# Attention block of a fused tokenizer, attention and expert kernel: softmax denominators as a column beside the values, weighted sums transposed back, divided, and transposed again

## What is computed

```python
qkv = (xn @ w_qkv + b_qkv).reshape(b, t, 3, H, hd)      # b=64, t=82, H=16, hd=16
scores = jnp.einsum('bhqd,bhkd->bhqk', q, k) * scale
attn = jax.nn.softmax(scores + bias, axis=-1)           # bias depends on q-k and the head
out = jnp.einsum('bhqk,bhkd->bhqd', attn, v)
out = jnp.transpose(out, (0, 2, 1, 3)).reshape(b, t, dim)
h = h + out @ w_out + b_out
```

## Time and profile before

| what | value |
|---|---|
| median of runs | 857.1 us |
| profiled execution: time, span | 861.1 us, 859.3 us |
| mean granted clock of TensorE over the span | 0.91 |
| busy: PE, PEld, DVE, ACT, POOL | 690.2, 527.5, 599.7, 349.9, 285.6 us |
| attention passes 0 to 63 | from 241.2 us to 657.0 us of the span |

### The profile page before, as it was taken

The page is one execution under the profiler, slowest core; times in us unless marked ns, Lnnn a source line. Parts: engine busy times, 40 slices in busy tenths (PEclk is TensorE's granted clock), DMA queues, the critical chain, the costliest instruction groups (busy, mean ns, idle before and its releaser), DMA issues. The chain is left out here.

```text
span 859.3 us, 24631 instructions
## 1 busy us (share of the span) xinstructions
PE 690.2 (80%) x10030; PEld 527.5 (61%) x10030; DVE 599.7 (70%) x1199; ACT 349.9 (41%) x793; POOL 285.6 (33%) x361
## 2 busy tenths in 40 slices
PE   1769696461479999999999999999988479999960
PEld 1657543320257777777777777777766368888850
DVE  0627657843459899999899998998885246766525
ACT  1211111000035555555555555555454335555533
POOL 2474200002272333333233333332000455667333
PEclk9879899675779999999999999999998769999995
DMA  8990100005910000000000000000000412222117
GB/s 158 225 311 8 37 1 0 1 12 178 306 23 8 15 16 14 15 16 21 14 9 21 15 15 16 15 15 15 21 14 15 98 56 74 71 81 76 51 65 272
DMA packets 34786, 51.42 MB, mean 60 GB/s; under 512 B 9044, under 2 KB 26292, under 8 KB 34548
## 3 DMA queue, kind: packets, MB, share of 16 engines
q1 hardware_dynamic: 29524, 39.57, 16.2%
q0 software_dynamic: 5152, 10.29, 4.2%
HBM read 36.91 MB, written 18.00 MB: 64 GB/s over the span
## 5 line engine op out<-in xcount | busy, mean ns | idle before, releaser
L934 ACT ACTIVATE probT<-psP 82x328 f32<-82x328 f32 x256 | 112.1, 438 | 161.4 <-PE psP L834 161.4
L993 DVE TENSOR_REDUCE mx<-psS 82x8 f32<-82x656 f32 x128 | 106.5, 832 | 42.4 <-PE psS L825 42.2
L834 PE MATMUL psP<-ident_all,prob 82*82 82x82 f32 x1024 | 117.3, 236 | 22.5 <-ACT probT L934 22.4
L834 PEld LDWEIGHTS psP<-ident_all,prob 82*82 82x82 f32 x1024 | 89.8, 120 | 65.6 <-issue 25.9
L755 POOL TENSOR_TENSOR h_flat<-h_flat,po 128x256 f32<-128x256 f32 x41 | 29.7, 725 | 263.7 <-ACT po L921 263.7
L995 DVE TENSOR_TENSOR prob<-psS,mx 82x656 f32<-82x656 f32 x128 | 107.1, 837 | 4.4
L926 ACT ACTIVATE prob<-prob 82x656 f32<-82x656 f32 x128 | 94.8, 741 | 3.1 <-DVE prob L995 3.1
L802 PE MATMUL psQ<-hT,early 128*128 128x328 f32 x256 | 83.1, 449 | 0.6 <-ACT hT L903 0.5
L1005 DVE RECIPROCAL rden<-psO 128x164 f32<-128x164 f32 x64 | 74.8, 1169 | 4.4 <-PE psO L852 4.4
L812 PE MATMUL psQ<-early,hT 128*82 128x256 f32 x256 | 66.7, 383 | 0.1
L825 PE MATMUL psS<-kT,qT 32*82 32x82 f32 x2048 | 53.6, 242 | 0.0
(11 more groups left out here) (218 smaller groups left out, 1216.5 us busy)
## 6 DMA issues: line engine op xcount, KB each, us to landing
img<-in_x SPq DMA_DIRECT2D x6, 1008.0 KB, 19.5
out<-h_flat SPq DMA_DIRECT2D x41, 128.0 KB, 2.5
fused_rows<-in_txt SPq DMA_DIRECT2D x1, 4928.0 KB, 25.1
h_flat<-entry_rows SPq DMA_DIRECT2D x6, 512.0 KB, 6.5
h_flat<-fused_rows SPq DMA_DIRECT2D x1, 2176.0 KB, 16.2
ex_w2a<-in_ff_w_A SPq DMA_DIRECT2D x1, 2048.0 KB, 11.2
ex_w1b<-in_ff_w_B SPq DMA_DIRECT2D x2, 1024.0 KB, 16.7
out<-h_flat SPq DMA_DIRECT2D x8, 256.0 KB, 4.8
```

Of the source, the lines that this page charges most:

```text
L834: mm = te.transpose(psP[0:T, s * T:s * T + T], prob[:, b % 2, g, s, :], ident_all[0:T, 0:T])
L934: act.activation(probT[:, b % 2, g, :, :].rearrange("p s t -> p (s t)"), psP[0:T, 0:4 * T], ACT.Copy).then_inc(S["probT_ready"], 1)
L993: v.tensor_reduce(mx[:, half, :, :], s4, X, ALU.max).then_inc(S["max_ready"], 1)
```

## The change

The values of a head now have 32 columns on the stationary side: 16 values and 16 ones (the memset of vv writes 1.0 and the copy fills the first 16). One matmul per head gives the sums and the denominator, and `one2` and its 16 matmuls are gone. The result in psO has channels on partitions; ACT copies it to oT, PE transposes it in four pieces of 128 columns back to psO (tokens on partitions), DVE takes the reciprocal of one column per head (82x16) and multiplies (82x256) into att, PE transposes that in two pieces, and ACT copies it to attT, where the projection reads it as before. On DVE normalise now stands ahead of read_qk.

The core of the diff:

```diff
-                te.wait_ge(S["att_ready"], b)
-                for t in range(2):
-                    for a in range(2):
-                        for g in range(HG):
-                            te.matmul(psO[32 * g:32 * g + 32, t * T:t * T + T], vv[:, b % 4, 4 * t + g, a, :],
-                                      probT[:, b % 2, g, 2 * t + a, :], start=(a == 0), stop=(a == 1), tile_position=(0, 32 * g))
-                for t in range(2):
-                    for a in range(2):
-                        for g in range(HG):
-                            mm = te.matmul(psO[32 * g:32 * g + 32, (2 + t) * T:(3 + t) * T], one2[:, a, :],
-                                           probT[:, b % 2, g, 2 * t + a, :], start=(a == 0), stop=(a == 1), tile_position=(0, 32 * g))
+                te.wait_ge(S["attT_ready"], b)
+                for h in range(NH):
+                    k, s = h % 4, h // 4
+                    mm = te.matmul(psO[32 * k:32 * k + 32, s * T:s * T + T], vv[:, b % 4, h, :],
+                                   probT[:, b % 2, h % 8 // 2, 2 * (h // 8) + h % 2, :], start=True, stop=True, tile_position=(0, 32 * k))
                 mm.then_inc(S["weigh_done"], 1)
+            def turn_back(b):
+                te.wait_ge(S["oT_ready"], b + 1)
+                for s in range(4):
+                    mm = te.transpose(psO[0:T, s * 128:s * 128 + 128], oT[:, s, :], ident_all[:])
+                mm.then_inc(S["back_done"], 1)
+            def turn_att(b):
+                te.wait_ge(S["att_ready"], b + 1)
+                for c in range(2):
+                    mm = te.transpose(psO[:, c * T:c * T + T], att[:, 8 * c:8 * c + 8, :].rearrange("p h d -> p (h d)"), ident_all[0:T, 0:T])
+                mm.then_inc(S["attT_ps"], 1)
             def project(n):
-                te.wait_ge(S["att_ready"], last_of[n] + 1)
+                te.wait_ge(S["attT_ready"], last_of[n] + 1)
...
+            def copy_oT(b):
+                act.wait_ge(S["weigh_done"], b + 1)
+                act.activation(oT[:].rearrange("p s t -> p (s t)"), psO[:, 0:4 * T], ACT.Copy).then_inc(S["oT_ready"], 1)
+            def copy_attT(b):
+                act.wait_ge(S["attT_ps"], b + 1)
...
+                    ins = act.activation(attT[:, :, a:a + size], psO[:, 0:2 * T].rearrange("p (c t) -> p c t", c=2)[:, :, lo:lo + size], ACT.Copy)
+                ins.then_inc(S["attT_ready"], 1)
...
             def normalise(b):
-                v.wait_ge(S["weigh_done"], b + 1)
...
-                v.reciprocal(rden[:], o3[:, 1, :, :]).then_inc(S["rden_ready"], 1)
+                v.wait_ge(S["back_done"], b + 1)
+                v.wait_ge(S["attT_ps"], b)
+                o3 = psO[0:T, :].rearrange("p (h e) -> p h e", h=NH)
+                v.reciprocal(rden[:], o3[:, :, HD:HD + 1]).then_inc(S["rden_ready"], 1)
                 v.wait_ge(S["rden_ready"], b + 1)
-                for a, lo, size in pieces(T * b, T, RA):
-                    ins = v.tensor_tensor(attT[:, :, a:a + size], o3[:, 0, :, lo:lo + size], rden[:, :, lo:lo + size], ALU.mult)
-                ins.then_inc(S["att_ready"], 1)
+                v.tensor_tensor(att[:], o3[:, :, 0:HD], rden[:].to_broadcast([T, NH, HD]), ALU.mult).then_inc(S["att_ready"], 1)
```

More of the change, by code:

```diff
@@ L682, in attention_block @@
         wrel = sb("wrel", [128, 2, 2, 2]); own = sb("own", [128, 2]); ownq = sb("ownq", [128, 2])
-        one2 = sb("one2", [T, 2, 32])
         bown = sb("bown", [128, 2, 4])
@@ L690, in attention_block @@
         qT = sb("qT", [128, 2, 2, 2, QT]); kT = sb("kT", [128, 2, 2, 2, QT])
-        vv = sb("vv", [T, 4, 8, 2, 32])
+        vv = sb("vv", [T, 4, NH, 32])
         mx = sb("mx", [T, 2, 2, 4])
         prob = sb("prob", [T, 2, HG, 4, T]); probT = sb("probT", [T, 2, HG, 4, T])
-        attT = sb("attT", [128, 2, RA]); rden = sb("rden", [128, 2, T])
+        oT = sb("oT", [128, 4, T]); att = sb("att", [T, NH, HD])
+        attT = sb("attT", [128, 2, RA]); rden = sb("rden", [T, NH, 1])
         po = sb("po", [128, 2, C])
@@ L710, in _ @@
             sp.dma_start(out_row[:], row(I["at_b_out"], 128)).then_inc(S["a_w_in"], 16)
-            for name, tile in (("qrel", qrel), ("kt0", kt0), ("kt1", kt1), ("wrel", wrel), ("own", own), ("one2", one2)):
+            for name, tile in (("qrel", qrel), ("kt0", kt0), ("kt1", kt1), ("wrel", wrel), ("own", own)):
                 sp.dma_start(tile[:], I[name]).then_inc(S["a_w_in"], 16)
@@ L729, in _ @@
             pool.memset(mhalf[:], -0.5).then_inc(S["mhalf2_set"], 1)
-            pool.memset(vv[:], 0.0).then_inc(S["vv_clear"], 1)
+            pool.memset(vv[:], 1.0).then_inc(S["vv_ones"], 1)
             pool.wait_ge(S["mhalf2_set"], 1)
@@ L772, in _ @@
             te.wait_ge(S["bvb_ready"], 1)
-            te.wait_ge(S["a_w_in"], 16 * 8)
+            te.wait_ge(S["a_w_in"], 16 * 7)
             for c in range(2):
@@ L882, in _ @@
                     qk(b // 4 + 1, b % 4)
+                if 0 <= b - 2 < NB:
+                    turn_back(b - 2)
                 if 0 <= b - 1 < NB:
@@ L886, in _ @@
                     val(b + 1)
+                if 0 <= b - 2 < NB:
+                    turn_att(b - 2)
                 if b < NB:
@@ L911, in copy_val @@
                     act.wait_ge(S["weigh_done"], b - 3)
-                v4 = bank(("val", b))[0:T, 0:C].rearrange("p (s a d) -> p s a d", s=8, a=2)
-                pair = vv[:, b % 4, :, :, :].rearrange("p s a (h d) -> p s (a h) d", h=2)[:, :, 0:4:3, :]
-                act.activation(pair, v4, ACT.Copy).then_inc(S["psQ_act"], 1)
+                act.activation(vv[:, b % 4, :, 0:HD], bank(("val", b))[0:T, 0:C].rearrange("p (h d) -> p h d", h=NH),
+                               ACT.Copy).then_inc(S["psQ_act"], 1)
+            def copy_oT(b):
[3 more added lines that the diff above has]
+                act.wait_ge(S["attT_ps"], b + 1)
+                done = (T * b + T - RA + 127) // 128
+                if done > 0:
+                    act.wait_ge(S["project_done"], done)
+                for a, lo, size in pieces(T * b, T, RA):
+                    ins = act.activation(attT[:, :, a:a + size], psO[:, 0:2 * T].rearrange("p (c t) -> p c t", c=2)[:, :, lo:lo + size], ACT.Copy)
+                ins.then_inc(S["attT_ready"], 1)
             def copy_project(n):
@@ L938, in _ @@
                 copy_xT(n)
-            act.wait_ge(S["vv_clear"], 1)
+            act.wait_ge(S["vv_ones"], 1)
             copy_val(0)
@@ L943, in _ @@
             for b in range(NB + 3):
+                if 0 <= b - 2 < NB:
+                    copy_oT(b - 2)
                 if 0 <= b - 1 < NB:
@@ L955, in _ @@
                     copy_val(b + 1)
+                if 0 <= b - 2 < NB:
+                    copy_attT(b - 2)
                 if b < NB:
@@ L1013, in _ @@
                 normal_stats(n)
-            v.wait_ge(S["a_w_in"], 16 * 8)
+            v.wait_ge(S["a_w_in"], 16 * 7)
             v.tensor_scalar(ownq[:], own[:], float(HD) ** -0.5, None, ALU.mult).then_inc(S["a_step"], 1)
@@ L1044, in _ @@
                     shift(b, 1)
+                if 0 <= b - 2 < NB:
+                    normalise(b - 2)
                 if b // 4 + 1 < NQ:
                     read_qk(b // 4 + 1, b % 4)
-                if 0 <= b - 2 < NB:
-                    normalise(b - 2)
                 for n in turned(b + 2):
@@ L1406, in shape_constants @@
     qrel, kt0, kt1 = (np.zeros((128, 2, T), np.float32) for _ in range(3))
-    own, one2 = np.zeros((128, 2), np.float32), np.zeros((T, 2, 32), np.float32)
+    own = np.zeros((128, 2), np.float32)
     for a in range(2):
-        one2[:, a, HD * a:HD * a + HD] = 1.0
         for g in range(HG):
@@ L1424, in shape_constants @@
             "upper": np.triu(np.ones((128, 128), np.float32), 1), "ident": np.eye(128, dtype=np.float32), "qrel": qrel, "kt0": kt0, "kt1": kt1,
-            "own": own, "one2": one2}
+            "own": own}
 def relative_rows(w_rel):
```

4 lines of the change are left out of this document (removed).

## The result

The changed kernel takes 893.8 us (median of 4 runs, 892.4 to 895.0), the kernel before 855.9 us beside it (4 runs, 854.7 to 864.0). The ratio is 1.042, with a 95% interval from 1.035 to 1.049: 4% slower. The forecast was 890 us, range 877 to 907.

The account below looks back on a forecast made before the run. DVE's read was taken to bound passes with a project, ACT those without; 23.0 + 5.8 + 3.3 + 1.0 = 33.1 us, on a median of 857.1, gave 890 us, range 877 to 907.

Parts of the forecast that it names:

- What bounds a pass: Attention passes with a project hang on DVE: shifts, reads, project, turn, scores, 6.62 us; those without hang on ACT.
- PE: -0.06 a pass, worth nothing: PE per pass: 0.68 us of ones matmuls go, transposes add 0.46 and 0.16; sum -0.06, nothing on PE.
- DVE's saving is worth nothing: DVE saves about 0.8 us a pass, but the old step stood behind the read with idle time after it.
- The new step: 0.64: New normalise ahead of DVE's read takes 0.64 us (reciprocal 0.25, product 0.43, less 0.04); 36 x 0.64 = 23.0 us.
- Passes without a project: turn_att waits for att, next scores at +6.61 against 6.39 (17 passes) or 6.20 (five); 5.8 us in all.
- The last passes: From pass 60 the project waits for copy_attT: 0.93 x 3 for 60, 62 and 63, 0.48 for 61; 3.3 us.
- Behind pass 63's scores: Pass 63's 0.93 us, plus the last two images without cover, 0.4 each, 1 us with a lower clock.
- Ahead of pass 2: At the block's start, one constant load less costs and gives nothing, since the tokenizer hides it.
- (a): Rival: PE's work is the bound and the change is faster, 9 us less, 848 us; 4%.
- (b): Rival: the new DVE step is hidden, adding 7 us or less, 857 to 864 us; 5%.
- (c): Rival: the small reciprocal, its source stepping 32 elements in PSUM, is slow; 77 us more, 967 us; 2%.
- (d): Rival: the clock falls to 1.2 GHz in one pass in ten, adding 30 us, 920 us; 3%.

Follow-up runs that it names:

- norm_first_in_before: The kernel before with only the old normalise moved ahead of read_qk on DVE; 974.6 us against 904.4, ratio 1.077.
- product_twice: The changed kernel with a second product of the same shape (82x256) into a spare tile ahead of the real one; 965.6 us, 1.067 of the kernel before.
- no_ones_in_before: The kernel before without the 16 matmuls on the ones per image, the same-shaped reciprocal reading the sums instead; 903.4 us against 904.4, ratio 0.998.
- small_recip_before: The kernel before, in its own order, with a reciprocal of 16 elements in place of 164; 904.6 us against 906.0, ratio 0.999.
- small_recip_between: The kernel before reordered with the read between the shifts, and a reciprocal of 16 elements in place of 164; 904.5 us, 0.997 of the kernel before.
- turn_att_late: The changed kernel with read_qk ahead of normalise, turn_att and copy_attT in the next pass, weigh, turn_back and copy_oT later; 867.4 us against 860.0 before, ratio 1.008.
- read_first_again: The changed kernel with read_qk put back ahead of normalise on DVE, nothing else; 984.7 us, ratio 1.091 to the kernel before.
- read_between_after: The changed kernel with DVE's read between the shifts, turn_att and copy_attT in the next pass, turn_back behind turn(b, 0); 849.6 us against 860.0 before, ratio 0.989.
- read_between_before: The kernel before with DVE's read between the shifts, PE's weigh behind turn(b-1, 3), second exponent later on ACT; 859.8 us against 860.0, ratio 1.001.

## Why the prediction was right, point by point

**What bounds a pass** held. The chain scores, shifts, read, project, turn, scores came out with the same intervals, and norm_first_in_before, product_twice and no_ones_in_before each moved one link of it or beside it and gave the pass to 0.02 us.

**PE: -0.06 a pass, worth nothing.** Right; the four transposes come 401.99 - 401.55 = 0.44 ahead of the next block (0.46 forecast). That even -0.68 would be worth nothing in a pass with a project is shown by no_ones_in_before.

**DVE's saving is worth nothing.** Right in this order (small_recip_before), and in the other one as well where PE's work stays (small_recip_between), which I hadn't expected.

**The new step: 0.64.** The reciprocal took 0.24 and the product 0.42 (0.25 and 0.43 forecast), the read moved by 0.61 to 0.62: 36 x 0.62 = 22.3 us for 23.0. Interpolating between a row for 8 elements and one for 164 held. The stepped source in PSUM cost nothing: 16 elements that lie side by side took 0.24 us too (small_recip_before). One sign came out smaller than I had said: PE waits 0.38 us for the read and not 0.5 to 0.7. In these passes too turn_att keeps turn(b, 0) back, which starts at 403.54 - 398.44 = +5.10 instead of +4.84, and I had PE at the project at +5.2. That doesn't change the sum, as the read ends last in either case.

**Passes without a project**: 6.55 for 6.61, since turn_att starts 403.34 - 403.28 = 0.06 behind the end of the product and not 0.15. That gives 17 x 0.16 + 5 x 0.35 = 4.5 us for 5.8. That turn_att holds up turn(b, 0) is shown by product_twice (0.33 more) and read_first_again (7.48), and turn_att_late gives the time back.

**The last passes**: a step that failed. I had the project of passes 60, 62 and 63 wait for copy_attT, +0.93 each. It reads an older image and doesn't wait: in pass 60 (scores at 657.28) of the changed kernel

```profile
662.18 0.36 PE L861 MATMUL psO<-ident_all,att 82*128 82x82 f32 x2 [1.01 <-DVE att L1035]
...
662.58 0.31 ACT L939 ACTIVATE attT<-psO 128x164 f32<-128x164 f32 x1
...
662.66 1.07 PE L870 MATMUL psQ<-wout,attT 128*128 128x256 f32 x4
```

the project starts at +5.38, in the middle of that copy, behind turn(b, 0). Passes 60 to 62 cost 1.5 us more (19.9 against 18.4), where the forecast was 0.93 x 2 + 0.48 = 2.3.

**Behind pass 63's scores** the term was too small: forecast 0.93 + 1.0, measured 22.1 - 16.6 = 5.5 us. PE waits at turn_att with nothing queued that it could do, and much of this stretch runs at half the clock, 1.2 GHz. The timeline, and then the stretch from the scores of pass 63 to the end of the last addition, in the kernel before and in the changed one:

```profile
682.11 0.54 PE L861 MATMUL psO<-ident_all,att 82*128 82x82 f32 x2 [1.88 <-DVE att L1035]
...
694.06 0.54 PE L861 MATMUL psO<-ident_all,att 82*128 82x82 f32 x2 [0.80 <-DVE att L1035]
```

```profile
651.17:667.79 16.62, 13.01 (x261) 9.91 (x260) 7.76 (x11) 5.46 (x12) 2.92 (x4) 0.79 0.08 26
677.21:699.31 22.10, 16.70 (x184) 12.29 (x182) 5.19 (x10) 7.98 (x20) 2.90 (x4) 0.61 0.05 19
```

The clock falls in both: from the means of 0.79 and 0.61, some 7 of the 16.6 us and 17 of the 22.1 run at the half. The longer chain of one image shows in every kernel that has it: 22.1, 21.0 and 22.5 us for the change, turn_att_late and read_between_after, against 16.6 and 18.2 for the kernel before and read_between_before. How much of the 5.5 us the chain makes and how much the clock was not tried.

**Ahead of pass 2** the changed kernel is 2.1 us shorter, which was counted as nothing, with the reason that the tokenizer hides the load of the constant. The trace before doesn't bear this reason out, since the first matmul of the block waits for that very load:

```profile
222.98 2.05 PE L775 MATMUL psO<-wout,bvb 128*128 128x256 f32 x4 [23.09 <-DMA one<-in_one]
```

After the change it starts at 220.95, behind the load of `own`, the last one then, with the same idle time of 23.13. But turn_att_late, which has no such load either, starts there at 223.06 and read_between_before, which has it, at 221.69. So what the load is worth can't be told from the spread between executions.

The errors nearly cancel, which is luck: -0.7, -1.3, -0.8 and +3.6 by stage, and -2.1 before pass 2. The sum of 33.1 us stands against 31.6 in the spans. The passes 2 to 59, four fifths of it, came out 2 us under their forecast and by the mechanism forecast.

**The rivals.** (a), PE as the bound, is shown to be wrong. (b), a hidden step, too. (c), a slow reciprocal, too. (d), the clock, was wrong for the passes, 1.00 from 300 to 640 us. Behind pass 63 it falls, in the kernel before as well, but for longer in the changed one; and it is what cost read_first_again most of what it took beyond its forecast. With six transposes more in each pass the clock stayed at its full level, so by this trace too the rule of the Trainium skill ("TensorE: Matmul & The Clock Gate", Part 4), that the full clock doesn't engage for transposes, does not describe what such a mix does.

## What to carry to other kernels

In a software pipeline written out by hand, price an instruction by what is queued behind it, not by its engine's busy share: here an engine at 74% passed every added 0.33 us on in full, and one at 95% gave nothing back for 0.68. When a change makes a step cheaper and also moves it, look at the move first: the saving of 0.9 us on DVE was worth nothing, and the place of the remaining 0.6 cost most of the 4%. And a change that lost in its own order can win in another: with the same steps, placed where no one waits for them, it came out 1.1% below the kernel before.

## What the runs showed of the hardware that I had not expected

- The granted clock can fall inside a loop in which PE is busy 259 of 300 us: 0.94 over that stretch in read_first_again, where it fell to half again and again. Ahead of one such fall, at 439.7, PE had idled 0.97 and 0.62 us at two places of the pass; passes of 8.30 to 8.39 stand beside ones of 7.48. In norm_first_in_before, with waits of 1.65 us and PE busy 250 of 300 us, it was 0.99. What makes the difference is open.
- The kernel before took 856 to 860 us in some sets of runs and 904 and 906 in two others, each on another chip. small_recip_before, whose passes should be its own, has 6.62, 6.39 and 6.20 us there; but its scores of pass 0 start at 267.35 us instead of 241.21, and its experts take 213.0 us instead of 191.5. These two make up the whole difference of the spans, 47.5 us, and the attention none of it. What makes them longer is open.
- A reciprocal of 16 elements that lie 32 apart in PSUM took 0.24 us, as long as one of 16 side by side, and the product over 16 runs of 16 elements, 82x256, 0.42.
